# Turning two groups' sums on VectorE in 32 x 32 blocks and placing them by transfers, in a cross-attention and mixture-of-experts kernel

## What is computed

```python
x = x + attention(layernorm(x), ctx)                       # x: 16 x 112 x 256, ctx: 16 x 375 x 256
n = layernorm(x)
g = einsum('bsh,ehf->ebsf', n, w_gate)                     # 8 experts, 256 -> 1024
u = einsum('bsh,ehf->ebsf', n, w_up)
h = silu(g) * u
expert_out = einsum('ebsf,efh->ebsh', h, w_down)           # 1024 -> 256
cw = softmax(n @ w_router) * softmax(n @ w_gating / 0.1); cw = cw / (sum(cw) + 1e-9)
out = x + einsum('ebsh,bse->bsh', expert_out, cw)
```

## Time and profile before

| | before |
|---|---|
| median of 3 runs | 970.96 us |
| the profiled execution's own time | 970.92 us |
| its span | 969.0 us |
| TensorE clock granted | 1.00 of full speed |
| TensorE busy | 964.6 us (100%) |
| VectorE busy | 737.2 us (76%) |
| GpSimd busy | 787.4 us (81%) |
| ScalarE busy | 484.8 us (50%) |
| DMA, 16 engines, queue of SyncE | 16.8% |

### The profile page before, as it was taken

The page is one execution under the profiler, slowest core; times in us unless marked ns, Lnnn a source line. Parts: engine busy times, 40 slices in busy tenths (PEclk is TensorE's granted clock), DMA queues, the critical chain, the costliest instruction groups (busy, mean ns, idle before and its releaser), DMA issues.

```text
span 969.0 us, 14845 instructions
## 1 busy us (share of the span) xinstructions
PE 964.6 (100%) x5164; PEld 895.6 (92%) x5164; DVE 737.2 (76%) x1264; ACT 484.8 (50%) x859; POOL 787.4 (81%) x626
## 2 busy tenths in 40 slices
PE   9999999999999999999999999999999999999998
PEld 7999899999999999999999999999999999999998
DVE  4986347777777877788878788777888777877886
ACT  7997554444545444444445444445445444444441
POOL 5999966767888888888988888888889888888852
PEclk9999999999999999999999999999999999999999
DMA  7441131411010110011100110011101100111202
GB/s 206 144 124 42 42 98 42 140 63 42 23 44 22 42 56 29 23 63 42 44 22 23 49 55 23 24 62 42 44 22 49 56 23 23 43 42 42 76 1 76
DMA packets 43490, 51.59 MB, mean 53 GB/s; under 512 B 3044, under 2 KB 39368, under 8 KB 43416
## 3 DMA queue, kind: packets, MB, share of 16 engines
q1 hardware_dynamic: 43408, 50.64, 16.8%
q10 hardware_dynamic: 8, 0.00, 0.0%
HBM read 45.07 MB, written 5.56 MB: 52 GB/s over the span
## 4 chain that ended last, share of the span: by engine, by line
PE 99%; DVE 0%; issue 0%; DVEq 0%
PE ps L324 96%; PE ps L1722 1%; PE ps L1831 1%; PE ps L1758 1%; PE ps L1710 0%; PE ps L1775 0%; PE ps L1801 0%; PE ps L1964 0%; PE ps L1668 0%; PE ps L1826 0%; DVE w_raw L1390 0%; DVEq L82 0%; DVE lg L1447 0%; PE ps L1674 0%; PE ps L1971 0%
## 5 line engine op out<-in xcount | busy, mean ns | idle before, releaser
L324 PE MATMUL ps<-arena 128*128 128x448 f32 (+5 forms) x2064 | 387.9, 339 | 0.0
L324 PEld LDWEIGHTS ps<-arena 128*128 128x128 f32 (+2 forms) x2064 | 343.5, 186 | 21.4 <-POOL arena L587 0.4
L593 POOL TENSOR_TENSOR arena<-shared,arena 128x448 fp32r<-128x448 f32 x196 | 252.8, 1303 | 132.9 <-ACT arena L965 125.3
L324 PE MATMUL ps<-xc_hi,w_hi 128*128 128x448 f32 x904 | 331.7, 367 | 0.0
L324 PE MATMUL ps<-xc_hi,w_lo 128*128 128x448 f32 x904 | 330.2, 365 | 0.0
L324 PE MATMUL ps<-xc_lo,w_hi 128*128 128x448 f32 x904 | 330.2, 365 | 0.0
L324 PEld LDWEIGHTS ps<-xc_hi,w_hi 128*128 128x128 f32 x904 | 169.8, 188 | 14.1 <-DVE cw_rows L1416 0.4
L324 PEld LDWEIGHTS ps<-xc_hi,w_lo 128*128 128x128 f32 x904 | 169.8, 188 | 13.6
L324 PEld LDWEIGHTS ps<-xc_lo,w_hi 128*128 128x128 f32 x904 | 169.9, 188 | 13.0
L958 ACT ACTIVATE shared<-shared 128x448 f32<-128x448 f32 x180 | 101.5, 580 | 146.0 <-DVE shared L1325 74.5
L710 POOL TENSOR_TENSOR xsacc<-xsacc,xf 128x448 f32<-128x448 f32 x104 | 119.2, 1158 | 0.0
(11 more groups left out here) (166 smaller groups left out, 1156.9 us busy)
## 6 DMA issues: line engine op xcount, KB each, us to landing
early<-in_L_ffn_w_down SPq DMA_DIRECT2D x16, 512.0 KB, 4.0
xf<-cw_dram SPq DMA_DIRECT2D x16, 448.0 KB, 4.7
shared<-in_ctx SPq DMA_DIRECT2D x16, 336.0 KB
w_raw<-in_L_ffn_w_gate SPq DMA_DIRECT2D x17, 256.0 KB, 2.8
w_raw<-in_L_ffn_w_up SPq DMA_DIRECT2D x17, 256.0 KB, 3.3
early<-in_L_ffn_w_gate SPq DMA_DIRECT2D x15, 256.0 KB, 2.7
early<-in_L_ffn_w_up SPq DMA_DIRECT2D x15, 256.0 KB, 3.0
xsacc<-in_x SPq DMA_DIRECT2D x8, 224.0 KB, 5.1
```

The costliest lines, as they stand in the source:

```text
L324: ins = nc.tensor.matmul(dst, w, m, start=first and i == 0, stop=last and i == len(passes) - 1, skip_group_check=onto)
L593: nc.gpsimd.tensor_tensor(h[:, 1, j, at:at + TC], tile, h[:, 0, j, at:at + TC].bitcast(fp32), ALU.subtract).then_inc(hid_lo_done, 1)
```

## The change

VectorE turns each sum of 128 x 448 in place in blocks of 32 x 32 (`turn`), eight instructions: four of half 0 in quad 61, four of half 1 in quad 62. A block is then turned inside, but stands in the wrong place. SyncE issues transfers that place the blocks (`place(cp, j)`): for each 32 partitions of the source (j), each of the two 128-column halves (d) and each of the four destination groups of 32 partitions (i), one transfer of 32 partitions x 7 x 32 elements, so 32 transfers a half and 64 in all, each of 28 KB in 224 runs of 128 bytes. Half 0 lands in the space of `last_acc[1]`, half 1 in the space of `acc`'s half 0. GpSimd adds them to `last_acc` tile by tile (`add_back`), 7 adds of 128 x 256 a half: half 0 in quad 62 ahead of `low_hidden(62, ...)`, half 1 at its very end. `load_last(1)` now waits until half 0's seven adds are done, since they read the space it fills. TensorE's `turn_back` and VectorE's `add_back` go. `down(30, 0)` moves in quad 62 from behind `up_4_3` to ahead of it, and `down(30, 3)` in quad 63 from ahead of `up_1_6_5` to behind `gate_2_7`.

```diff
+    Q = 32
+    BACKS = DK * (P // Q) ** 2
+        back = [last_acc[1], acc[:, 0:RT, :]]
...
+            def load_last(cp):
                 sp.wait_ge(acc_stored[cp], DMA)
                 sp.dma_start(last_acc[cp], x1_tiles[:, cp * RT:(cp + 1) * RT, :]).then_inc(last_in[cp], DMA)
+            def place(cp, j):
+                for d in range(DK):
+                    for i in range(P // Q):
+                        src = acc_t[j * Q:(j + 1) * Q, cp, d, :].rearrange("s (t i e) -> s t i e", i=P // Q, e=Q)[:, :, i, :]
+                        at = d * P + j * Q
+                        sp.dma_start(back[cp][i * Q:(i + 1) * Q, :, at:at + Q], src).then_inc(back_in[cp], DMA)
+            sp.wait_ge(w_done, FPAIRS * SETS - 1)
+            load_last(0)
+            sp.wait_ge(w_done, FPAIRS * SETS)
+            sp.wait_ge(turned_done[0], UNITS)
+            for j in range(P // Q):
+                place(0, j)
+            sp.wait_ge(turned_done[1], UNITS)
+            sp.wait_ge(back_in[0], BACKS * DMA)
+            place(1, 0)
+            place(1, 1)
+            sp.wait_ge(back_done[0], RT)
+            load_last(1)
+            place(1, 2)
+            place(1, 3)
...
+            def add_back(cp):                                       # GpSimd
+                pool.wait_ge(back_in[cp], BACKS * DMA)
+                pool.wait_ge(last_in[cp], DMA)
+                for i in (range(RT), (4, 5, 0, 1, 2, 3, 6))[cp]:
+                    to = last_acc[cp][:, i, :]
+                    nc.gpsimd.tensor_tensor(to, to, back[cp][:, i, :], ALU.add).then_inc(back_done[cp], 1)
...
+                if n == QUADS - 2:
+                    add_back(0)
                 low_hidden(n, HID11, g11, 0, 0)
...
+            def turn(cp, k):                                        # VectorE
+                ve.wait_ge(unit_done, UNITS * (len(TURNED) - 2 * CP + cp) + k + 1)
+                to = unit_at(GROUPS - 2 * CP + cp, k)
+                nc.vector.transpose(to, to).then_inc(turned_done[cp], 1)
...
                 up_u2(n)
+                if n == QUADS - 3:
+                    for k in range(UNITS):
+                        turn(0, k)
                 if n == QUADS - 2:
-                    add_back(0, 1)
+                    turn(1, 0)
...
-                    add_back(0, 2)
-                if n == QUADS - 1:
-                    add_back(1, 0)
+                    turn(1, 1)
+                    turn(1, 2)
...
                 hidden22(n)
+                if n == QUADS - 2:
+                    turn(1, 3)
...
-            def turn_back(cp, i):                                   # TensorE
...
-                        ins = nc.tensor.transpose(to, acc_t[:, cp, block, t * P:(t + 1) * P], ident[:])
-                ins.then_inc(back_ready[cp], 1)
```

More of the change, by code:

```diff
@@ L238, in xattn_ffn_kernel @@
         ps_unit = [ps[:, 6 + i, 0:TC] for i in range(2)]
-        ps_back = [[ps[:, 6 + i % 2, :] for i in range(RT // 2)] + [ps[:, 7, 0:D]],
-                   [ps[:, 6, :], ps[:, 7, :], ps[:, 0, :], ps[:, 7, D:2 * D]]]
         ps_cw = ps[0:TILES * E, 5, 0:P]
@@ L289, in xattn_ffn_kernel @@
         acc_stored, last_in = [sem("acc_stored0"), sem("acc_stored1")], [sem("last_in0"), sem("last_in1")]
-        back_ready, back_done = [sem("back_ready0"), sem("back_ready1")], [sem("back_done0"), sem("back_done1")]
+        turned_done, back_in, back_done = [[sem(f"{n}{cp}") for cp in range(CP)] for n in ("turned_done", "back_in", "back_done")]
         PARTS = {"first": (A11, slice(0, 3, 2), 2), "second": (A21, slice(1, 4, 2), 2), "s13": (S1, slice(4, 6), 2),
@@ L480, in _ @@
                     load_cw(e, 1)
-            for cp in range(CP):
-                sp.wait_ge(w_done, FPAIRS * SETS - 1 + cp)
+            def load_last(cp):
                 sp.wait_ge(acc_stored[cp], DMA)
                 sp.dma_start(last_acc[cp], x1_tiles[:, cp * RT:(cp + 1) * RT, :]).then_inc(last_in[cp], DMA)
+            def place(cp, j):
[18 more added lines that the diff above has]
+            place(1, 3)
             sp.wait_ge(acc_done, RT * (CP + 1))
@@ L748, in _ @@
             low_hidden(QUADS - 1, HID12, u12[1], 1, 0)
+            add_back(1)
         @block.scalar
@@ L1386, in add_rows @@
                 if g >= CP:
-                    ve.wait_ge(back_done[g % CP], i // 2 + 1)
+                    ve.wait_ge(back_done[g % CP], (i, (2, 3, 4, 5, 0, 1, 6)[i])[g % CP] + 1)
                     to = last_acc[g % CP][:, i, :]
@@ L1405, in weigh @@
                 nc.vector.tensor_tensor(to, ps_unit[u % 2], cw_all[:, g % CP, c * TC:(c + 1) * TC], ALU.mult).then_inc(weighed_done, 1)
[L1407 to L1412, removed]
+            def turn(cp, k):
+                ve.wait_ge(unit_done, UNITS * (len(TURNED) - 2 * CP + cp) + k + 1)
+                to = unit_at(GROUPS - 2 * CP + cp, k)
+                nc.vector.transpose(to, to).then_inc(turned_done[cp], 1)
             def keep_cw():
@@ L1617, in quad @@
                     add_rows(g - 1, 5, ps_r[5])
+                up_u2(n)
+                if n == QUADS - 3:
+                    for k in range(UNITS):
+                        turn(0, k)
                 if n == QUADS - 2:
-                    add_back(0, 0)
-                up_u2(n)
-                if n == QUADS - 2:
-                    add_back(0, 1)
+                    turn(1, 0)
                 if odd and g in TURNED:
@@ L1653, in _ @@
             add_rows(GROUPS - 2, 5, ps_r[5])
-            add_back(1, 2)
-            ve.wait_ge(back_ready[1], 4)
             add_rows(GROUPS - 2, 6, ps_r[6])
-            add_back(1, 3)
             for i, made in ((4, 2), (5, 2), (0, 4), (1, 4), (2, 6), (3, 6), (6, RT)):
@@ L1948, in unit @@
                 accumulate(ps_unit[u % 2], passes).then_inc(unit_ready, 1)
-            def turn_back(cp, i):
[L1952 to L1963, removed]
-                        ins = nc.tensor.transpose(to, acc_t[:, cp, block, t * P:(t + 1) * P], ident[:])
-                ins.then_inc(back_ready[cp], 1)
             def turn_cw():
@@ L1985, in down @@
                 if i % 2 == 0:
-                    if g == GROUPS - CP and i in (0, 2):
-                        pe.wait_ge(back_done[0], 3 + i // 2)
+                    if g == GROUPS - CP and i < 4:
+                        pe.wait_ge(weighed_done, UNITS * len(TURNED) - 1 + i // 2)
                     elif g == GROUPS - CP:
-                        pe.wait_ge(back_done[1], i // 2 - 1)
+                        pe.wait_ge(acc_done, RT * CP + i - 2)
                     else:
@@ L2163, in quad @@
                     down(g - 1, 5)
[L2164 to L2167, removed]
                 up_1_6_5(n)
@@ L2172, in quad @@
                     unit(g, 2)
-                if n == QUADS - 2:
-                    turn_back(0, 1)
                 gate_2_7(n)
-                if odd and by_tile and n < QUADS - 1:
+                if odd and by_tile:
                     down(g, 3)
[L2178 to L2181, removed]
                 up_2_7(n)
-                if n == QUADS - 2:
-                    turn_back(0, 3)
                 gate_4_3(n)
@@ L2189, in quad @@
                     unit(g, 0)
-                if n == QUADS - 1:
-                    turn_back(1, 1)
+                if n == QUADS - 2:
+                    down(g, 0)
                 up_4_3(n)
@@ L2197, in quad @@
                 if not odd and by_tile:
-                    down(g, 0)
+                    if n < QUADS - 2:
+                        down(g, 0)
                     down(g, 1)
@@ L2207, in _ @@
             down(g, 5)
-            pe.wait_ge(act_done, last + HID11)
-            turn_back(1, 2)
             down(g, 6)
-            turn_back(1, 3)
             g = GROUPS - 1
```

4 lines of the change are left out of this document (removed).

## The result

The changed kernel takes 974.89 us, the median of its runs; the kernel before took 971.37 us beside it. The ratio is 1.0037, with a 95% interval from 1.0023 to 1.0051. It is slower by about 3.6 us, where 3.1 us faster was forecast, and the time lies above the range of 967.2 to 972.0.

What follows compares the result with a forecast made beforehand. TensorE, busy 964.6 of 969.0 us, was taken as the bound. Removing 3.08 us of transposes from 970.92 with nothing new late gave 967.84, forecast 967.8 us, with an 8-in-10 range of 967.2 to 972.0.

Steps and rivals of the forecast that it cites:

- What bounds the kernel, and the 3.08 us: In TensorE's sequence near the end: removing the transposes of L1964 saves 3.08 us, all on the path.
- VectorE's turns: On VectorE in quad 61: half 0's four turns at 0.53 us each, 2.1 us, fit in 2.36 us of idling.
- rival B: On VectorE: a turn takes 1.09 us, giving 969.0 us in all; at 1.48 us a turn about 971.5; chance 0.13.
- SyncE's transfers, half 0: On SyncE from 917.6 us: 32 issues 0.51 us apart, the last at 933.4, landed 2.1 later at 935.5 us.
- Whether the engines keep up: On the DMA engines: 128-byte packets between 10 and 27 ns, 0.14 to 0.38 us a transfer, below the issue's 0.51.
- Rival A: On the DMA engines: the transfers set the pace, 971.7 us at 0.63 us apart, 980.5 at 0.77; chance 0.21.
- GpSimd's adds: In quad 62: half 0's seven adds take 5.2 us, delaying `low_hidden` by 4.1; half 0 may land as late as 938.2.
- VectorE beside GpSimd, and the moved tiles: In quad 62: one or two hidden products grow from 0.6 to 1.5 us, at worst 0.5 lost; moved tiles cost nothing.
- Half 1: At the end: transfers start about 936.3, land at 954.7 us, GpSimd's adds through at 960.0, with 2.9 us of room.
- Rival C: In quads 62 and 63: the loop through VectorE, ScalarE and GpSimd bounds, waits replace the transposes, 970.9 us; chance 0.06.

## Why the prediction was wrong, point by point

**What bounds the kernel, and the 3.08 us.** Right. The versions in which the blocks land in time take 967.48, 967.51, 967.65 and 967.62 us, against 967.84 in the sum; the span goes from 969.0 to 965.8 us.

**VectorE's turns.** Right. Four took 2.21 us and one 0.62, so 0.53 apart, and `weigh(29, 2)` followed without delay. The estimate of 1.09 us, scaled from the Trainium skill (VectorE: DVE Perf Modes, The three transpose paths), was too high; rival B falls.

**SyncE's transfers, half 0.** This is the step that failed, and two of the signs that the prediction gave for being wrong are there: issues 0.6 us or more apart, and GpSimd's last add ahead of the last `add_rows`. The step took 0.51 us from one issue to the next out of the earlier trace rows, "the shape nearest". The shape was near, but shape hardly matters. What matters is where the two ends lie, and the text itself noted that the trace had no transfer from SBUF to SBUF, only to use that for the packets and not for the issue. 31 x (0.65 - 0.51) is 4.3 us of the 6.6 us by which half 0 was late. The rest: the start 0.2, a first issue 0.14 longer, a pause of 0.3 in the row of issues, and the last landing, 3.6 us behind its issue instead of 2.1.

That last landing has a cause of its own in the trace. A transfer has 240 packets here, its 224 runs and 16 small ones at the end. Of the last transfer 225 had started by 940.4 us, and 15 only afterwards. Just ahead of those 15 a packet of 16 KB for instructions ran. The queues' packets, MB and share of the 16 engines, from 939.4 to 940.4 us and from 940.4 to 941.5:

```profile
q1 hardware_dynamic: 225, 0.03, 16.8%
q8 instruction: 1, 0.02, 9.1%
...
q1 hardware_dynamic: 15, 0.00, 2.6%
```

0.091 x 16 engines x 1 us is 1.46 us for that one packet. 15 packets are one engine's share of the transfer, so they most likely stood behind it; the trace does not name the engine. The run with half 1 merged shows the same, with a packet of 0.073 x 16 = 1.2 us and a landing at 3.55 us. Without it half 0 would have landed about 1.7 us earlier, still 2 us after the last good moment.

**Whether the engines keep up.** Right, and it misled. Of the kernel after, 920 to 930 us:

```profile
DMA packets 3684, 0.44 MB, mean 44 GB/s; under 512 B 3684, under 2 KB 3684, under 8 KB 3684
...
q1 hardware_dynamic: 3684, 0.44, 27.1%
```

0.271 x 16 x 10 us / 3684 = 12 ns a packet, between the 10 and 27 ns that were given, so 0.17 us a transfer. The doubling that the rule of the Trainium skill (DMA: Bandwidth & Descriptors, Specifications) would have meant is not there. Its section Why small descriptors are slow (HBM only) gives other reasons than reading and modifying, so it doesn't bear on that rule as the prediction used it; whether small packets inside SBUF are free of a penalty, as it says, no run settles: 128 bytes in 12 ns are 11 GB/s an engine, and the 1 KB packets of the earlier trace rows made 23. But the upper bound of the distance, 0.63 us, was worked out from the engines alone. No bound from above was put on the issue itself, for which the trace had no transfer with the same ends. The measured 0.65 lies just outside.

**Rival A.** Its formula was right: the point of decision at 0.62 us and "by 0.65 about 973". The changed kernel is 2 us beyond, the 2 us of pause and landing that the formula did not have. But its mechanism was not this one: it had the DMA engines' packets set the pace, at 0.63 or 0.77 us, and the rows on packets, which spoke against that, made its chance small. They say nothing of the issue.

**GpSimd's adds.** Right in size (4.92 and 5.32 us against 5.2; 6.11 in the run out of DRAM), and the deadline was right: L1382 was the first to wait, and with half 0 landing 3.9 us after the last good moment, 938.2, TensorE stood 3.17 us. What was not in the sum is the clock. Five stretches of the kernel after:

```profile
946.00:950.00 4.00, 0.83 (x5) 0.44 (x4) 1.28 (x4) 1.01 (x2) 4.00 (x5) 0.93 0.29 47
949.00:949.50 0.50, 0.00 (x0) 0.00 (x0) 0.20 (x1) 0.21 (x1) 0.50 (x2) 0.94 0.35 57
950.00:951.00 1.00, 1.00 (x3) 0.91 (x4) 1.00 (x2) 0.00 (x0) 1.00 (x2) 0.50 0.24 38
952.50:953.00 0.50, 0.50 (x5) 0.50 (x4) 0.50 (x2) 0.50 (x2) 0.15 (x1) 0.65 0.31 49
953.00:953.50 0.50, 0.50 (x6) 0.50 (x6) 0.50 (x2) 0.30 (x1) 0.50 (x1) 1.00 0.35 57
```

The granted clock fell to 0.50 at 949.44 us, while TensorE stood, and was 1.00 again at 952.85, 2.9 us after it had gone on. Its first six matmuls came 0.37 us apart instead of 0.20, the first 0.54 before the second, and took 2.40 us instead of 1.21: 1.2 us more.

**VectorE beside GpSimd, and the moved tiles.** Right, at no cost. In the first version with both halves merged, whose adds run at that time, two hidden products of quad 62 grew, from 0.60 and 0.61 us in the kernel after:

```profile
937.46 0.95 DVE L1408 TENSOR_TENSOR shared<-shared 128x448 f32<-128x448 f32 x1
938.34 1.57 DVE L1413 TENSOR_TENSOR shared<-shared 128x448 f32<-128x448 f32 x1
```

and TensorE shows no wait behind them.

**Half 1.** The room of 2.9 us was right as far as the versions whose blocks land in time show it. In the kernel after it landed 10.5 us later than worked out: 5.8 from its start, at 942.1 with half 0's landing instead of 936.3, the rest from 32 issues at 0.14 more. It alone sets the end there.

**Rival C** falls: TensorE's count of instructions was the bound, as the versions whose blocks land in time show.

Open is what makes an issue with both ends in SBUF longer. Open, too, are the pauses: of 0.3 us in half 0's row, and one issue of 0.98 us at 962.9 in the kernel after, which like the two of 1.08 and 1.07 us in the run with half 0 merged began 0.3 to 0.4 us after such a packet for instructions had begun.

## What to carry to other kernels

This chain of small transfers was paced by its issues, not by the engines that move the bytes. So take the price of an issue from a transfer with the same ends, not with the same shape, and bound it from above by itself when there is none. When a plan needs tens of transfers before a deadline, multiply the error of one by their number: 0.14 us was 4.3 us after 32. And put more into each: laying out the landing buffer so that two block columns share one distance halved the issues at no cost and turned 3.6 us lost into 3.3 to 3.6 us gained.

## What the runs showed of the hardware

- An issue on SyncE with both ends in SBUF takes 0.61 us, with one end in DRAM, on either side, 0.45 us, both 0.04 us apart from the next. From 32 to 448 runs it grows from 0.59 to 0.63 us; with 896, where the DMA engines were 96% busy, it was 0.67.
- SyncE's issues still take 0.61 us while ScalarE issues at the same time, at 0.64.
- Packets of 128 bytes inside SBUF take 12 ns of an engine.
- A packet of 16 KB for instructions took 1.5 us of one engine, in another run 1.2, and the transfer issued before it landed 3.6 us after its issue, where the median is 1.9.
- VectorE turns 128 x 448 in fp32 in 32 x 32 blocks in 0.62 us, 0.53 us apart in a row, like an add that reads PSUM.
- TensorE came back from 3.17 us of standing at half its clock, and was at full clock again 2.9 us later.
